# A two-layer decoder block on one core: the kernel padding, the keys and values and the attention of the first layer written as one block

## The reference, cut to what matters

```python
def _L0_attn_ref(hidden_states, Wq, bq, Wk, bk, Wv, bv, Wo):
    H, KVH, D, EPS = 16, 4, 128, 1e-06
    q = hidden_states @ Wq.T + bq        # 512 -> 2048
    k = hidden_states @ Wk.T + bk        # 512 -> 512
    v = hidden_states @ Wv.T + bv
    sq = elu(q) + 1.0                    # per head
    sk = elu(k) + 1.0                    # each k/v head serves 4 query heads
    kv = jnp.einsum('bhsd,bhse->bhde', sk, v)
    qkv = jnp.einsum('bhsd,bhde->bhse', sq, kv)
    norm = jnp.einsum('bhsd,bhd->bhs', sq, sk.sum(axis=2))
    attn = qkv / (norm[..., None] + EPS)
    return attn @ Wo.T                   # 2048 -> 512
...
x = _layernorm(x + _L0_attn_ref(x, ...))
x = _layernorm(x + _L0_xattn_ref(ctx_2048, ctx_2048, x, L0_xattn_ssm_kernel, L0_xattn_D, 8))
x = _layernorm(x + _L0_ffn_ref(x, ...))
...   # three more sublayers of the second layer
```

## Time and profile before

| what | value |
|---|---|
| median of three runs | 2037.88 us |
| the three runs | 2034.43, 2037.88, 2043.33 us |
| span of the profiled execution | 2041.2 us |
| PE busy in it | 1832.9 us (90%) |
| DVE, ACT, POOL busy in it | 1253.9, 918.1, 290.8 us |
| DMA queue q1 | 134.52 MB, 23.2% of 16 engines |

### The profile page before, as it was taken

One profiled execution on the slowest core, in us unless ns is written; L12 is line 12 of the kernel. 1 busy time (PEld: TensorE's weight loads), 2 busy tenths in 40 slices (PEclk: granted clock), 3 DMA queues, 4 the chain that ended last, 5 costly groups with the idle time before them and its releaser, 6 DMA issues. The chain is left out here.

```text
span 2041.2 us, 33020 instructions
## 1 busy us (share of the span) xinstructions
PE 1832.9 (90%) x12272; PEld 1493.2 (73%) x12272; DVE 1253.9 (61%) x2330; ACT 918.1 (45%) x2376; POOL 290.8 (14%) x347
## 2 busy tenths in 40 slices
PE   6979999999997889999999987899997698889966
PEld 5868999999885778888888885677775455555543
DVE  3446444444447656555654536788887587778847
ACT  2225333333334443333333214676666587778811
POOL 0000000000012111111111001333334112111001
PEclk9989999999999999999999998999997899899988
DMA  3022000000014221101110013000013575665134
GB/s 106 32 95 92 21 22 22 22 21 1 22 53 129 83 73 42 47 19 40 48 37 17 11 42 124 12 32 32 32 53 96 148 170 147 151 150 127 49 118 142
DMA packets 86253, 136.62 MB, mean 67 GB/s; under 512 B 9480, under 2 KB 25480, under 8 KB 86096
## 3 DMA queue, kind: packets, MB, share of 16 engines
q1 hardware_dynamic: 86096, 134.52, 23.2%
HBM read 79.88 MB, written 21.05 MB: 49 GB/s over the span
## 5 line engine op out<-in xcount | busy, mean ns | idle before, releaser
L2224 ACT ACTIVATE e_p<-e_s_ps,e_nb 128x512 f32<-128x512 f32 x256 | 175.1, 698 | 45.5 <-DVE e_nb L2270 43.7
L2270 DVE TENSOR_REDUCE e_nb<-e_s_ps 128x2 f32<-128x1024 f32 x128 | 155.8, 1218 | 51.2 <-PE e_s_ps L2346 50.5
L1710 ACT ACTIVATE p<-p,nb,rq 128x128 f32<-128x128 f32 (+1 forms) x256 | 136.9, 541 | 92.9 <-DVE nb L1811 92.9
L2356 PE MATMUL e_t_ps<-ident,e_p 128*128 128x128 f32 x1024 | 147.7, 283 | 21.2 <-DVE e_pT L2277 13.5
L894 PE MATMUL yp<-ccy,toep 128*128 128x288 f32 x600 | 159.1, 413 | 5.7 <-ACT ccy L876 3.6
L2356 PEld LDWEIGHTS e_t_ps<-ident,e_p 128*128 128x128 f32 x1024 | 120.1, 146 | 58.9 <-issue 49.6
L80 PE MATMUL q_ps<-a_xt_hi,wq_hi 128*128 128x256 f32 x512 | 151.3, 296 | 4.1 <-DVE wo_lo L112 4.1
L1231 DVE SCALAR_TENSOR_TENSOR hm<-gu_ps,us_col,sg 128x256 f32<-128x256 f32 x88 | 42.3, 481 | 177.4 <-ACT sg L1120 177.4
L82 PE MATMUL q_ps<-a_xt_hi,wq_lo 128*128 128x256 f32 x512 | 145.7, 285 | 0.0
L81 PE MATMUL q_ps<-a_xt_lo,wq_hi 128*128 128x256 f32 x512 | 145.4, 284 | 0.0
L527 ACT ACTIVATE ex<-ex 128x512 f32<-128x512 f32 x64 | 40.4, 632 | 213.1 <-DVE ex L590 213.1
(11 more groups left out here) (300 smaller groups left out, 5151.7 us busy)
## 6 DMA issues: line engine op xcount, KB each, us to landing
x_after<-n_r SPq DMA_DIRECT2D x24, 512.0 KB, 3.0
toep<-padded_kernels SPq DMA_DIRECT2D x32, 256.0 KB, 3.6
qs<-e_xh SPq DMA_DIRECT2D x64, 128.0 KB, 2.5
qs<-e_xl SPq DMA_DIRECT2D x64, 128.0 KB, 2.6
ks<-e_ch SPq DMA_DIRECT2D x64, 128.0 KB, 2.6
ks<-e_cl SPq DMA_DIRECT2D x64, 128.0 KB, 2.7
x<-x_after SPq DMA_DIRECT2D x12, 512.0 KB, 4.5
x<-in_x SPq DMA_DIRECT2D x8, 512.0 KB, 4.0
```

The lines of the kernel that those rows point to most:

```text
L1710: act.activation(p[n % 3][:, h, part[t]], p[n % 3][:, h, part[t]], ACT.Exp, bias=nb[i][:, t, h:h + 1], scale=rq[u][:, t:t + 1], accum_out= ...
L2224: act.activation(pr[i][:, a, :], s_ps[i][:, a, :], ACT.Exp, bias=nb[i][:, a:a + 1], accum_out=sums[t][:, j, q:q + 1]).then_inc(e_done, 1)
L2270: dve.tensor_reduce(nb[i][:], s_ps[i][:], AX.X, ALU.max, negate=True).then_inc(nb_done, 1)
L2356: last = pe.transpose(t_ps[a][:, k, :], pr[m % 2][:, a, k * P:(k + 1) * P], core.ident[:])
```

## The change

The blocks `pad_kernels`, `l0_keys_values` and `l0_attention` become one block, `l0_front`.

1. **No barriers between the three.** The zeroing of `kpad`, its two loads, its add and its store are still there. SP issues the loads behind the loads of the keys' weights, DVE adds at the end of batch 1 of the keys, and SP issues the store behind the load of batch 3 of x. SP waits for its landing after the last weight piece of the block.
2. **Sixteen turned batches in one series.** x is turned 16 times in a row, the eight batches for keys and values and then the eight for attention (`v % B`), with one pair of x buffers. PE turns batch 0 of the attention between the value projections of batch 7, where the kernel before turned nothing.
3. **Wq and Wo split beside the keys.** Of 16 pieces, 12 (all of Wq, the first half of Wo) are split at the end of batches 1 to 6 of the keys, two each, on ACT and DVE behind their other work of that batch. SP loads two pieces behind the load of x from batch v = 4 on. The four late pieces of Wo are split in steps 0 to 3 of the first attention batch, one each: on ACT between the exponential and the scaling, on DVE behind the maximum.
4. **The last `products`** (batch 7) runs behind the first query projection of the attention, and its copy on ACT behind the first exponential.
5. **Shared memory.** Wk lies in the second half of `wo_hi`, Wv in the second half of `wo_lo`; `kb` shares a tile with `ex`, the two bias rows lie in the norm's tile `n_r`; `k_ps`, `v_ps` and `kv_ps` are the banks of `q_ps`, `a_ps` and `o_ps`. ACT therefore waits for the last value projection before it splits a late piece.

The core of the diff:

```diff
+LATE_PIECES = 12
+def qo_order(q, o):
+    half = H0 // 4
+    return [(f, p) for p in range(half) for f in (q, o)] + [(f, p) for f in (q, o) for p in range(half, 2 * half)]
+def q_piece(p):
+    return 2 * p if p < H0 // 4 else H0 // 2 + p - H0 // 4
+def o_piece(p):
+    return 2 * p + 1 if p < H0 // 4 else LATE_PIECES + p - H0 // 4
...
+        def early_pieces(b):
+            return (2 * b - 2, 2 * b) if 1 <= b <= LATE_PIECES // 2 else (0, 0)
+        def load_x(sp, v):
+            sp.dma_start(xt.x[v % 2][:], rows(x, v % B)).then_inc(xt.loaded[v % 2], 16)
...
             def _(sp):
+                split_kv.load(sp)
+                sp.dma_start(bk_row, bk.partition_broadcast(P)).then_inc(bias_loaded, 16)
+                sp.dma_start(bv_row, bv.partition_broadcast(P)).then_inc(bias_loaded, 16)
+                load_x(sp, 1)
                 sp.dma_start(bq_col[:], bq).then_inc(bq_loaded, 16)
-                split.load(sp, 0, 4)
-                xt.load(sp, 1, 1)
-                split.load(sp, 4)
+                sp.wait_ge(pad_zeroed, 1)
+                sp.dma_start(kpad[:, PAD:PAD + D], kernel).then_inc(pad_loaded, 16)
+                sp.dma_start(dcol, dskip).then_inc(pad_loaded, 16)
+                sp.wait_ge(split_kv.lo_done, len(split_kv.pieces))
+                ahead.load_weights(sp)
+                for v in range(2, B + 2):
+                    sp.wait_ge(xt.turned, 2 * v - 2)
+                    load_x(sp, v)
+                    if v == 3:
+                        sp.wait_ge(pad_added, 1)
+                        sp.dma_start(padded, kpad).then_inc(pad_stored, 16)
+                    if v >= 4:
+                        split.load(sp, 2 * v - 5, 2 * v - 3)
+                split.load(sp, 2 * B - 1)
+                sp.wait_ge(pad_stored, 16)
...
             def _(act):
+                for b in range(B):
...
+                    xt.round_hi(act, b + 1, (b + 1) % 2, [1])
+                    split.round_hi(act, *early_pieces(b))
...
                     for p, attend, _ in steps(b, first):
                         n = NP * b + p
-                        if first and p < NP - 1:
-                            split.round_hi(act, 2 * p + 2, 2 * p + 4)
                         act.wait_ge(mq_done, 2 * n + 2)
-                        act.activation(ex[p % 2][:], ex[p % 2][:], ACT.Exp).then_inc(eq_done, 1)
+                        act.activation(ex[p % 2], ex[p % 2], ACT.Exp).then_inc(eq_done, 1)
+                        if first and p == 0:
+                            copy_kv(B - 1)
+                            act.wait_ge(v_mm, T * B)
+                        if first and p < len(split.pieces) - LATE_PIECES:
+                            split.round_hi(act, LATE_PIECES + p, LATE_PIECES + p + 1)
...
             def _(dve):
...
+                    if b == 1:
+                        dve.wait_ge(pad_loaded, 32)
+                        dve.tensor_tensor(kpad[:, PAD:PAD + 1], kpad[:, PAD:PAD + 1], dcol, ALU.add).then_inc(pad_added, 1)
...
+                    split.take_lo(dve, *early_pieces(b))
...
+                        if first and p < len(split.pieces) - LATE_PIECES:
+                            split.take_lo(dve, LATE_PIECES + p, LATE_PIECES + p + 1)
...
             def _(pe):
...
+                for b in range(B):
...
+                    for t in range(T):
+                        xt.turn(pe, b + 1, (b + 1) % 2, [t])
+                        project(wv, v_ps, v_mm, v_done, b, b % 2, [t])
+                pe.wait_ge(kb_done, T * B)
...
                         if first:
-                            pe.wait_ge(split.lo_done, 2 * p + 2)
+                            pe.wait_ge(split.lo_done, q_piece(p) + 1)
                         project_q(b, u, p)
+                        if first and p == 0:
+                            products(B - 1)
...
         constants(core, to_kv)
-        pad_kernels(core, ssm_kernel, d_skip, padded)
...
-                l0_keys_values(core, to_kv, to_attention, kv, x, bk, bv)
-                l0_attention(core, to_attention, to_mixer, kv, x, between[0], bq, cv)
+                l0_front(core, to_kv, to_attention, to_mixer, kv, x, between[0], bk, bv, bq, ssm_kernel, d_skip, padded, cv)
```

260 lines of the change are left out of this document (102 added, 158 removed).

## The result

The changed kernel took 2017.43 us in the median (2010.22 to 2019.71 us), the kernel before, run beside it, 2038.31 us: a ratio of 0.9898, with a 95% interval of 0.9868 to 0.9929. The forecast was 2017.2 us. A second series of the same two kernels gave 2013.54 us and 2036.67 us, 0.9892 [0.9874, 0.9911]. The change brings 1%, 21 to 23 us.

A forecast was written before the change was run, and what follows sets the result against it. PE was taken as the bound, with three holes in front of it that the change fills: 7.9 + 0 + 12.4 + 0 + 0.4 = 20.7 us, from the median 2037.88 to 2017.2 us; range 2011.5 to 2026 us.

The forecast's parts named there:

- The start: Before the first turn of x: with the padding off the path it begins at 4.54 instead of 12.45 us.
- The batches: Keys and values, batches 1 to 6: two added weight pieces per batch stay hidden on DVE and ACT, cost 0.
- The second piece is issued behind the load of x, at T + 1.1: Batches of keys: the second weight piece lands at T + 5.7 and is subtracted at T + 8.0.
- T: Zero point for times within a batch of keys and values: the second turn of that batch.
- The spare of 1.2 us: DVE in batches of keys: gap between key biases done, T + 9.4, and the minimum's start, T + 10.7.
- the rival of the late piece: Batches 2 to 6: the second piece lands late in each, costing 3 to 10 us, 2020 to 2028 us; chance 0.13.
- The boundary: Keys to attention: first attention turn comes at M + 11.5 instead of M + 25.0, less 1.1 us for turning; gain 12.4 us.
- M: Time at which DVE sees the last value projection (last value bias), 130.40 us in the kernel before.
- The clock: First turn of an attended pair: after 3.0 us of waiting PE's clock falls as before; gain 0, other end 2.0 us.
- The rival that the clock stays up: Behind PE's 3.0 us wait at the first attention turn the clock does not fall; time 2015.2 us, chance 0.16.
- the row with 2.56 us: Earlier trace: a 2.56 us wait followed by a slow turn of 1.12 us at 137.41 us, cited for the fall.
- The rest of batch 0: Later steps of the first attention batch: fewer weight pieces left to split; gain 0.4 us (0 to 0.6).

The follow-up runs named there:

- the late pieces behind: Changed kernel with the four late pieces split in steps 1 to 4, behind the turned pair's rounding (ACT) and low part (DVE); 2017.88 us, ratio 0.9913.
- the kernel with the padding block: Changed kernel with one part undone: pad_kernels is its own block again, ahead of everything; 2023.08 us, ratio 0.9929.
- the kernel with the loads later still: Changed kernel with the second piece of batches 2 to 6 loaded behind the value biases of its own batch; 2024.19 us in one run.
- after: The changed kernel itself, all parts of the change against the kernel before; 2017.43 us, ratio 0.9898; second series 2013.54 us, 0.9892.

## Why the prediction was right, point by point

**The start, 7.9 us: right.** 7.94 us by the first turn, 8.05 us by the first key matmul. The first turn waits for x alone, and that x lands 3.8 us after its issue could be read from the earlier trace rows. The padding, moved beside the keys, costs nothing that the timeline shows; the edit done alone on the kernel before moved the first key matmul by 8.00 us and the first turn of a pair by 8.22 us.

**The batches, 0 us: right in the result, wrong in one step.** The step "The second piece is issued behind the load of x, at T + 1.1" is wrong. SP waits for `xt.turned` at 2v - 2 before `load_x`, and the pieces of that turn of the loop belong to the next batch of splits: their loads are issued a batch ahead, as soon as the place in `ring` is given back (42.92 us). I had numbered the batches off by one between the loop of SP and that of ACT. The spare of 1.2 us was therefore put too small: DVE is done with the pieces at T + 6.4, not T + 8.0. The step's own arithmetic can be checked where its premise is true: with the loads moved to where I had thought them, the batch shown came out to 0.2 us in every time of the list, and the periods stayed at 13.82 us. Its edge was near, for one of the five pieces landed 5.8 us after its issue, where the prediction let the loss begin. So the rival of the late piece had no ground in this kernel, and when made real by a later load it cost 2.6 us in all, below its 3 to 10 us.

On the order of landings, a page of the Trainium skill ("DMA: Bandwidth & Descriptors", section "Queues, rings and completion order") had stood as the reason for a late piece. Of the five pieces moved to T + 1.07 none was overtaken: they landed 4.6 to 5.8 us after their issue, each ahead of the piece issued behind it. But loads are overtaken elsewhere, and there the trace agrees with the page. With the late pieces behind, x was issued at 12.68 us and the padding's kernel, an eighth of its size, at 13.67 us; their sizes and times to landing:

```profile
a_x<-in_x SPq DMA_DIRECT2D x1, 512.0 KB, 9.5
...
kpad<-in_ssm_kernel SPq DMA_DIRECT2D x1, 64.0 KB, 6.6
```

The padding's kernel landed at 20.3 us, x at 22.2 us, and it is this x that PE waited 1.45 us for.

**The boundary, 12.4 us: right, 12.4 us.** 25.04 us from M to the turn became 11.12 us (predicted 11.5 us, bounds 8.5 us and later), and M itself lost 1.54 us (predicted 1.1 us): 25.04 - 11.12 - 1.54 = 12.4 us. The two deviations cancel. It is M + 11.12 and not M + 11.5 since piece 12 is subtracted at M + 7.54 (130.20 + 1.23 us; 7.8 predicted) and scaling and turn follow the minimum by 3.57 us (3.69 predicted). Of the 1.54 us, 1.19 us lie behind the second turn of batch 0 (100.20 us to M, before 99.01 us); the turning is 1.09 us of them, by the kernel that turns behind the values, and 1.1 us was predicted. The other 0.35 us is the first batch, from the first key matmul to its second turn: 11.42 us, before 11.07 us (31.39 - 20.32), with two more matmuls at the lower clock level. The chain named in the prediction (piece 12 on DVE, minimum, exponential, piece 13 on ACT, scaling, turn) is the one in the timeline, row by row.

**The clock, 0 us: the fall came, but that was partly luck; its price was short by 0.5 us.** The wait was 2.71 us (predicted 3.0 us), and the granted clock of the 4.09 us behind it was 0.60. The step to the second turn took 8.62 us, before 9.13 us, and 7.11 us in the kernel with the padding block, where the clock stayed up: the fall costs 1.5 us in this execution. I had left it at 2.0 us, and in the kernel with the loads later still the step took 9.84 us, a price of 2.7 us. The prediction took the fall for settled by the length of the wait. The runs show that length does not settle it: behind the same wait of 2.71 us the clock fell in five profiles and stayed up in two (the table below). The rival that the clock stays up was therefore no worse founded than the forecast's choice, and which of the two the medians hold is not known, since only one execution of each run has a profile. Nor was the row with 2.56 us that I had set against the rival a like case: two more waits of PE, of 0.83 and 1.00 us, stand just ahead of it (131.19 and 134.22 us in before).

**The rest of batch 0, 0.4 us: about right.** 0.7 us (from 20.94 to 21.65), and 0.3 us more up to the convolution, where I had put nothing.

**The sum.** 20.7 us predicted, 22.0 us at the convolution (the start 0.1 us more, the clock 0.5 us, the rest 0.6 us), 20.9 us in the median. That the median agrees to 0.2 us is partly chance: the unchanged part alone differed by 6.4 us between two profiles of the same kernel, and the medians of after in two series by 3.9 us. The range of 14.5 us was wide enough for either. Its lower end is 0.2 us off its own sum: 2015.2 - 3.5 is 2011.7 us, not 2011.5 us.

## What to carry to other kernels

Cost a merged block by following one engine's first instruction past the old barrier, down to the first value that someone waits for; the averages (DVE 45% busy) say nothing about it. Put the preparation of the next stage (here the turning, 4.4 us) beside the last full work of the bound engine; moving ten weight splits from the steps to the keys and four more off the start of the steps, much the larger edit, brought some 1 us, since the steps had hidden them. And where a load is issued from one engine's loop and used in another's, write down for one value which pass of each loop it belongs to before costing its arrival.
